# Four heads in four row groups of the array, with unused products over all rows in front of the row pairs

## The reference

```python
q = (x @ wq.T).reshape(B, S, 16, 8); k, v likewise       # 16 heads of 8
probs = softmax(einsum('bqhd,bkhd->bhqk', q, k) / sqrt(8))
out = einsum('bhqk,bkhd->bqhd', probs, v) @ wo.T
...
we = sum(where(sel == e, rw, 0))                          # top 2 of 8 experts
out += (silu(x @ w1[e].T) * (x @ w3[e].T)) @ w2[e].T * we
```

## Time and profile before

| | |
|---|---|
| median of 3 runs | 1235.07 us (1224.66 to 1239.53) |
| profiled execution | 1228.6 us, its span 1226.8 us |
| mean granted TensorE clock | 0.914 of full speed |
| busy: PE, DVE, ACT, POOL | 82%, 68%, 54%, 34% of the span |
| projection / attention / expert stage | 0 to 227, 227 to 985, 985 to 1227 us |

### The profile page before, as it was taken

One profiled execution on the slowest core, in us unless ns is written; L12 is line 12 of the kernel. 1 busy time (PEld: TensorE's weight loads), 2 busy tenths in 40 slices (PEclk: granted clock), 3 DMA queues, 4 the chain that ended last, 5 costly groups with the idle time before them and its releaser, 6 DMA issues. The chain is left out here.

```text
span 1226.8 us, 21943 instructions
## 1 busy us (share of the span) xinstructions
PE 1005.9 (82%) x5592; PEld 472.9 (39%) x5592; DVE 836.2 (68%) x1286; ACT 666.3 (54%) x1382; POOL 418.3 (34%) x767
## 2 busy tenths in 40 slices
PE   0156666999999999999999999999999968777850
PEld 0034442333333344344344344434443235554530
DVE  5667658789888778888888888888884013232552
ACT  1001111577777677777777777777776534333320
POOL 6103310010110143433433523524522434644576
PEclk9978776899999989999999999999998579988985
DMA  8954566010100110100101101101100012212342
GB/s 269 383 190 137 137 172 172 1 36 10 36 26 10 37 28 10 44 25 20 43 11 33 43 10 35 43 10 35 44 1 2 17 36 64 73 50 70 96 130 71
DMA packets 61944, 81.56 MB, mean 66 GB/s; under 512 B 8512, under 2 KB 39488, under 8 KB 61504
## 3 DMA queue, kind: packets, MB, share of 16 engines
q1 hardware_dynamic: 45808, 51.93, 14.8%
q10 hardware_dynamic: 11984, 20.59, 4.6%
q0 software_dynamic: 4096, 8.40, 2.3%
HBM read 32.12 MB, written 48.23 MB: 65 GB/s over the span
## 5 line engine op out<-in xcount | busy, mean ns | idle before, releaser
L1084 DVE TENSOR_REDUCE smax<-ps 128x2 f32<-128x1024 f32 x512 | 601.7, 1220 | 96.7 <-PE ps L1273 93.5
L853 ACT ACTIVATE prob<-ps 128x512 f32<-128x512 f32 x1024 | 528.8, 603 | 160.2 <-PE ps L1322 157.5
L1322 PE MATMUL ps<-qpack,kpack 34*128 34x512 f32 x1024 | 383.8, 458 | 23.6 <-ACT prob L853 11.7
L1273 PE MATMUL ps<-kpack,qpack 34*128 34x512 f32 x1024 | 314.2, 452 | 10.0 <-DVE smax L1084 9.3
L1322 PEld LDWEIGHTS ps<-qpack,kpack 34*128 34x128 f32 x1024 | 172.9, 189 | 297.2 <-ACT prob L853 250.2
L1332 PE MATMUL ps<-prob,vpad 128*32 128x512 f32 x2048 | 284.7, 629 | 0.0
L1273 PEld LDWEIGHTS ps<-kpack,qpack 34*128 34x128 f32 x1024 | 138.3, 189 | 41.3 <-DVE smax L1084 28.5
L450 POOL MEMSET qpack<- 2x2048 f32 x32 | 57.6, 1799 | 207.9 <-PE ps L1322 205.2
L1190 DVE TENSOR_TENSOR prob<-ps,prob 128x256 f32<-128x256 f32 x80 | 33.9, 424 | 104.9 <-ACT prob L906 104.0
L1498 PE MATMUL ps<-w,ws 128*128 x160 | 89.1, 642 | 15.3 <-ACT ws L899 14.5
L906 ACT ACTIVATE prob<-ps 128x256 f32<-128x256 f32 x80 | 30.8, 385 | 86.3 <-PE ps L1498 86.3
(11 more groups left out here) (211 smaller groups left out, 881.4 us busy)
## 6 DMA issues: line engine op xcount, KB each, us to landing
by_expert_rows<-prob ACTq DMA_DIRECT2D x4, 4864.0 KB, 30.9
q_parts<-qk SPq DMA_DIRECT2D x32, 256.0 KB, 3.8
k_parts<-qk SPq DMA_DIRECT2D x32, 256.0 KB, 4.0
kpack<-k_parts SPq DMA_DIRECT2D x32, 256.0 KB, 3.9
qpack<-q_parts SPq DMA_DIRECT2D x64, 128.0 KB, 3.3
vall<-by_expert_rows SPq DMA_DIRECT2D x80, 64.0 KB, 1.8
by_expert_rows<-vall SPq DMA_DIRECT2D x80, 64.0 KB
w<-w_t SPq DMA_DIRECT2D x3, 1024.0 KB, 10.1
```

The costliest lines, as they stand in the source:

```text
L853: act.activation(prob[:, v % RING, :], bank(col_bank(pos, kind)), ACT.Exp).then_inc(col_free, 1)
L1084: dve.tensor_reduce(smax[:, half, :, pair, qt, kh], ps[:, first:first + 2, :], AX_X, ALU.max).then_inc(row_free, 1)
L1273: ins = pe.matmul(bank(first + par), qpack[r:r + ROWS, slot, half, pair, qt * P:(qt + 1) * P], kpack[r:r + ROWS, slot, pair, kh * HALF:(kh ...
L1322: pe.matmul(bank(col_bank(pos, kind)), kpack[r:r + ROWS, slot, head // 2, kt * P:(kt + 1) * P], qpack[r:r + ROWS, slot, half, head // 2, : ...
```

## The change

CROSS becomes 24: three products of parts for four (low with low is left out), still with two rows for the maxima. Each head has its own 32-partition row group. Row pairs run over the 24 rows alone, so the clears go. In front of each row pair outside the opening, `keep_busy` issues one or two bfloat16 products over all 128 rows whose result the row pair overwrites. The last column product of a group moves, with the extra items, to the start of the next group, behind W. W's four increments become one. The seed on DVE and one of three Newton rounds go, for a power step on POOL. `save_x` runs one tile earlier.

```diff
-PARTS = 2
-CROSS = PARTS * PARTS * HD
+TERMS = 3
+CROSS = TERMS * HD
-ODD = 64
+LANE = 32
-PACK = 16 * 6
+PACK = 16 * 3 * HQ
...
 def save_parts(b):
+  if part == 0:   # both places of the high part in one DMA
+      both = (0, 2, 1) if w == 0 else (0, 3, 2)
...
+  else:
+      o = 2 if w == 0 else 1
+      sp.dma_start(rows[o * LANE:o * LANE + LANE, :], whole).then_inc(parts_out, 16)
 def load_k(n, slot):
-    for par in range(2):
+    for h in range(HQ):
+        sp.dma_start(kpack[LANE * h:LANE * h + CROSS, slot, :].bitcast(F32),
+                     of_head(k_parts, n, h)).then_inc(pack_in[slot], 16)
...
 def place_maxima(slot, half):
+    for part in range(PARTS):
+        sp.dma_start(qpack[CROSS + part:P:LANE, slot, half, :].bitcast(F32),
+                     mtr[16 * part:16 * part + 16, :]).then_inc(m_placed, 16)
...
-            def clear_maxima(slot):
...
+            gp.memset(kpack[:, :, :].bitcast(F32), 1.0).then_inc(pads, 1)
...
 def refill(i, slot, base, kind):
-    gp.wait_ge(col_full, base + (col_pos(UNITS - 1, kind) + 1))
-    gp.wait_ge(vpad_in, 2 * i + (2 + slot))
+    gp.wait_ge(pv_done, i * (2 * UNITS) + ((slot + 1) * UNITS + RING))
     gp.sem_inc(passed, 1)
-    clear_maxima(slot)
...
+                step(gp.tensor_tensor(rstd, var, power[:, :], ALU.pow))
...
-                gp.wait_ge(f_seed, t + 1)
-                for _ in range(3):
+                for _ in range(2):
...
-                if j % 4 == 3 and j + 1 < TILES_T:
+                if j % 4 == 2 and j + 2 < TILES_T:
                     save_x(j // 4 + 1)
...
+            def keep_busy(n, b):
+                for _ in range(n):
+                    pe.matmul(bank(b), busy[:, 0:P], busy[:, :], start=True, stop=True)
 def score_rows(p, slot, base, opening=False):
-    half, pair, qt, kh = p // 16, p % 16 // 8, p % 8 // 2, p % 2
+    half, pair, qt, kh = p // 16, 1 - p % 2, p % 16 // 4, p % 4 // 2
...
+    if not opening:
+        keep_busy(1 + p % 2, first)
+    for n in range(2):
+        r = (2 * pair + n) * LANE
+        ins = pe.matmul(bank(first + n), qpack[r:r + CROSS, slot, half, qt * P:(qt + 1) * P],
+                        kpack[r:r + CROSS, slot, kh * HALF:(kh + 1) * HALF], start=True, stop=True)
...
 def weigh_values(g, slot, base, kind):
-    ... .then_inc(pv_done, 1)
+    ins.then_inc(pv_done, HQ)
...
+            def last_of(g, job, slot, base, kind, t=None):
+                score_cols(4 * g + 3, 4 * g + 4, slot, base, kind)
+                for name in EXTRA[kind].get(g, ()):
...
 def group(g, i, slot, base, kind, before=None, t=None, opening=False):
+    if g > 0:
+        last_of(g - 1, job, slot, base, kind, t)
+    elif not opening:
+        last_of(15, job - 2, 1 - slot, *before)
...
     def rows(k):
...
+        else:
+            if g == 4 and k == 0:
+                pe.wait_ge(row_free, O_LAST)
+            keep_busy(1 + k, 2 - row_banks(O_LAST))
-    score_cols(4 * g, 4 * g + 1, slot, base, kind)
     rows(0)
-    score_cols(4 * g + 1, 4 * g + 3, slot, base, kind)
+    score_cols(4 * g, 4 * g + 2, slot, base, kind)
     rows(1)
-    score_cols(4 * g + 3, 4 * g + 4, slot, base, kind)
+    score_cols(4 * g + 2, 4 * g + 3, slot, base, kind)
     ...   # W of the group before, as it was
```

More of the change, by code:

```diff
@@ L344, in place_maxima @@
-            def place_maxima(slot, half):
[L346 to L350, removed]
+                            rows = dram[bass.ds(b * (NQ * TERMS * LANE) + j * (TERMS * LANE), TERMS * LANE), :]
+                            whole = qk2[LANE * j:LANE * j + LANE, w, part, :].bitcast(F32)
@@ L430, in _ @@
             gp.memset(ones[:, :], 1.0).then_inc(consts, 1)
+            gp.memset(power[:, :], -0.5).then_inc(consts, 1)
+            gp.memset(busy[:, :], 1.0).then_inc(consts, 1)
             gp.iota(iota_t[:, :], pattern=[[1, TILES_A]], base=0, channel_multiplier=0,
@@ L445, in _ @@
             gp.tensor_copy(run[:, 4, :], ebase[:, 0, :]).then_inc(consts, 1)
[L447 to L457 removed]
+            gp.memset(kpack[:, :, :].bitcast(F32), 1.0).then_inc(pads, 1)
+            gp.memset(vpad[:, :, :, :, :], 0.0).then_inc(pads, 1)
             gp.wait_ge(pads, 2)
[L459 to L461 removed]
             gp.memset(vpad[:, :, :, :, HD:HD + 1], 1.0).then_inc(pads, 1)
@@ L1143, in _, with dve_quad @@
             start += 2
-            def dve_quad(i, slot, own, last=False, t=None):
+            def dve_quad(i, slot, own, last=False):
                 base = i * (2 * ROW_ITEMS) + slot * ROW_ITEMS
@@ L1156, in dve_quad @@
                     split_maxima(0, following + (pair_pos(15) + 1), own + 3)
-                    maxima(16, 20, following)
-                    if t is not None:
-                        seed(t, own + 5)
-                    maxima(20, PAIRS - 2, following)
-                    finish_o(quad, 1, following + (O_LATE + 1), row_banks(O_LATE), own + (5 + extra))
+                    maxima(16, PAIRS - 2, following)
+                    finish_o(quad, 1, following + (O_LATE + 1), row_banks(O_LATE), own + 5)
                 else:
@@ L1165, in dve_quad @@
                     finish_o(quad, 1, O_LAST + 2, FINAL_BANK, own + 3)
-            with loop(dve, 0, 2) as i:
+            with loop(dve, 0, QUADS // 2 - 1) as i:
                 own = i * (2 * PER_QUAD) + start
@@ L1270, in score_rows @@
                     pe.wait_ge(row_free, base + (pos - 1))
-                for par in range(2):
-                    r = par * ODD
-                    ins = pe.matmul(bank(first + par), qpack[r:r + ROWS, slot, half, pair, qt * P:(qt + 1) * P],
-                                    kpack[r:r + ROWS, slot, pair, kh * HALF:(kh + 1) * HALF], start=True, stop=True)
+                if not opening:
[4 more added lines that the diff above has]
+                                    kpack[r:r + CROSS, slot, kh * HALF:(kh + 1) * HALF], start=True, stop=True)
                 ins.then_inc(row_full, 1)
```

126 lines of the change are left out of this document (46 added, 80 removed).

## The result

The changed kernel takes 1348.83 us (median of 4 runs, 1345.99 to 1351.42) where the kernel before, on the same chip, takes 1230.79 us (1224.66 to 1239.53): a ratio of 1.0953, with a 95% interval from 1.0871 to 1.1034. The profiled execution took 1351.42 us, its span is 1349.6 us, its mean clock 0.908. Against the profiled execution of before that is +122.8 us, where the forecast was +112.

What follows compares the result with a forecast made beforehand. The prediction took a loop through TensorE and ACT, 2.71 us per group, to bound the kernel. It summed 1228.6 + 134 - 14 - 8 = 1341 us, with an 8-in-10 range from 1205 to 1372.

Steps and rivals of the forecast that it cites:

- The mechanism: Attention groups: changes of array shape around the unused products make TensorE the bound, 3.23 us per group instead of 2.70.
- Rival 1: Between a group's moved last column and its third column: switches around unused products are free, 0 per group, 1207 us; chance 0.22.
- The passes: Attention groups outside the opening: shape changes and unused products add 0.53 us in each of 253 groups, +134 us.
- D: Block of one unused product, behind the moved last column: weight load, stream and drain take 0.36 us.
- DD: Block of two unused products, ahead of a group's second row pair: takes 0.58 us.
- the extra items add what they added: 0: Maxima, projection and logits, now between the moved last column and the first unused product: no additional cost, 0.
- The clock: Last quad: unused products keep the higher clock level, -14 us; the other hole gives 0, or -5 if it goes.
- The term of the last quad: Last quad, without row pairs: unused products keep the higher level, a group taking 2.70 us instead of 4.06, -14 us.
- The opening has no dummies: Opening of attention: it gets no unused products; no cost was put on it.
- the hole in quad 4: Lower clock after a stall ending at 422.20 us, which the change leaves: 0, or -5 if it goes.
- rival 3: Attention: the clock falls despite unused products, as 24-row products fill less; 5.75 us per group, +126 more, 1467 us; chance 0.06.
- The expert stage: Behind attention: earlier save_x, no DVE seed, fewer saved copies and Newton steps give about -8 us, bounds -13 and +1.

Runs made afterwards that it cites:

- the last one: Kernel before plus the expert edits and a block of two unused products in the last quad alone; 1310.89 us against 1337.99, ratio 0.9818.

## Why the prediction was right, and by how much its terms were off

**The mechanism** is the one forecast: TensorE became the bound through its changes of shape, and the marks named for it are there. Period 3.15 (forecast 3.23), 0.42 after c3' (0.43), idle time of DVE per maximum 233.5 / 512 = 0.46 us (0.4), no wait of TensorE for ACT before c2. The kernel without the blocks (2.69) and the one with blocks of the pair's shape (2.69) show that neither the layout nor the number of products is the cause. Rival 1 (free switches) is refuted by the rows above: a block costs its streams and some 0.10 us, where rival 1 needed switches under 0.02 us each.

**The passes, +134 forecast, about +120 measured.** The thirteen quads at full clock cost 7.5 us each where 16 x 0.53 is 8.5; sixteen of them would be 120. Two errors of size hide in that. D takes 0.32 and DD 0.53, not 0.36 and 0.58: entry and exit of a block are 0.32 - 0.215 = 0.105 us together, not the 0.15 that I read off float32 transposes. The plain period rose by 0.455 instead of 0.53 (115 us over 253 groups), and groups whose passes had slack before rose by only 0.3 to 0.4 (2.78 to 3.16 where one quad follows another). Against that stands the step "the extra items add what they added: 0". It was wrong: the groups with a turn rose from 2.91 to 3.66, 0.29 more than the others, which comes to about 5 us in the thirteen quads at full clock, since a turn beside other items cost less. I had followed the semaphores and TensorE's order, and not counted the ring's banks: an item that takes one between c3' and c0 makes c1 wait for the first exponential in place of c2. The experiment with the items first gives the 0.29 back (3.37), and those thirteen quads as a whole 4.3 us.

**The clock, -14 forecast, about +15 measured.** The term of the last quad was right: 49.2 us at 1.00; 15 won. Two steps failed. "The opening has no dummies" was read as no cost. In quad 0 the clock fell at 224 and came back at 275: eight groups of 5.55 us or more and a ninth of 4.38, instead of 3.15, +21. And for the hole in quad 4 I had written 0 or -5; it cost 9 more: it began with a shorter stall (1.12 us at 474.55, where before had 2.40) and lasted from 476.5 to 510.7, with groups of 5.55 to 7.44. This is rival 3's fall of the clock in two places; that it comes from the fewer rows isn't shown. Its period at the lower level was given as 5.75 and is 5.55, and I counted on full-array products to shut it out everywhere, though in the opening there are none. Nor do they bring the clock back soon once it is lost: in quad 0 they run from 231.7 on, and it stayed at 0.50 for 43 us more, TensorE busy for 97% of the window:

```profile
229.10:275.20 46.10, 44.80 (x159) 10.67 (x161) 21.60 (x21) 19.61 (x36) 0.00 (x0) 0.50 0.02 5
```

The kernel without unused products shows how close it was: without them the fall is the rule. The Trainium skill, "TensorE: Matmul & The Clock Gate" (Part 1), has the throttled state as the default that activity releases. The trace agrees in its direction; that an engine busy 94% of the time stays in it (the kernel without unused products) is this case's finding. What sets off the fall in the opening stays open.

**The expert stage, -8 forecast, -9.9 measured.** TensorE's waits for ACT before L1498 of before (14.5 us, 18 times) are one of 0.9 us at L1477 now, and POOL's 64 loads stay as long a queue (60.6 us busy and 32.8 idle; the earlier trace rows have 60.8 and 35.7). The power step takes 1.05 us, between the 0.20 and the 2 assumed. On one chip the stage took 247.3 us in the kernel before with unused products, and 232.6 and 233.5 in the two kernels with the expert edits (clock 0.83, 0.82 and 0.83). That speaks for the edits and against a mere shift of the rows' arrival, though the first of the three is from the traced execution of 1547.73 us; the one run with the edits alone was clouded by its chip, and which of them brings the gain wasn't tried apart. The stage also depends on the quad in front of it. The last quad and the stage of the kernel with the items first and products of the pair's shape:

```profile
956.30:1013.10 56.80, 56.00 (x298) 18.00 (x300) 7.89 (x13) 32.91 (x67) 24.38 (x59) 0.64 0.03 11
1013.10:1241.20 228.10, 153.50 (x788) 99.44 (x788) 82.95 (x226) 73.12 (x194) 130.51 (x240) 0.82 0.28 79
```

With the same edits and no long stalls the stage takes 235.6 us behind a last quad of 43.3, 231.8 behind 49.2, 228.1 behind 56.8 and 221.3 behind 72.9: a shorter last quad gives about half of its gain back. Behind a last quad as long as before's 56.6 the edits are thus worth 13 to 14 us (241.7 to 228.1), at the lower bound of -13, and since the last quad is 7.4 us shorter than before's, some 4 us are lost again here. Which work carries over isn't shown. **The projection stage**, 0 with bounds of -3 and +4, gave -2.3.

**The sum.** 134 - 14 - 8 = +112 against +122.8: passes -14, clock +29, expert stage -2, projection -2. The total lies near by luck, in part: two errors of opposite sign stood against each other; the clock's was the larger. Had the clock done as I wrote, the kernel would have taken some 1320 us.

## What to carry to other kernels

An unused product of another shape has three prices: its stream (0.215 us here), the entry into and exit from its block (0.10 us), and the work beside it that it cuts apart (two passes where one stood); give it a place with slack, in one block and not in two, and count which bank of a ring each moved item takes. A change of layout like this one can cost the clock, and a busy share of 94% gave no warning of it: look at the granted clock by window, in the openings and tails above all, where the filling work is missing. Before crediting a remedy such as this, cost the part of the kernel that it doesn't reach.

## What the runs showed of the hardware

**Rows and the clock.** In all ten traces of kernels with the 24- and 26-row products (nine kernels) attention began at the lower level (first period 4.06, clock 0.50 from between 224.0 and 227.4 on). The four with 34-row products (before, with unused products, with the expert edits, and the last one) began it at 1.00 (first period 2.60 or 2.61). The opening (the row pairs ahead of quad 0 and the first group) has no unused products in any of them. How long the lower level lasted differed: to 238 or 239 with one block of two, to 242 with one product in front of every row pair, to 251 and 275 with the same three products, to 256 and 306 with the 24-row ones, to 270 with one product in every second place, to 408 with none. Nor is it sure at the end: the last quad was at 1.00 in the changed kernel and fell (period 5.53) in the one with the items first, which has the same unused products. The two groups of kernels differ in more than the rows (row groups, order, clears), and no run tried the rows alone. Why, and what in the products the clock answers to, isn't settled.

**Chips.** The kernel before took 1235 and 1238 us on two of the four chips of the experiments, and 1356 and 1338 on the two others. On these two, the five kernels traced all had long stalls at the turn of the loop over quads, most of them in every second quad. ACT and TensorE in the last experiment's kernel, in one of them:

```profile
725.73 0.27 ACT L827 ACTIVATE mtr<-ps 32x128 f32<-32x128 f32 x1 [3.60 <-remote]
...
726.05 0.79 PE L1325 MATMUL ps<-qpack,kpack 34*128 34x512 f32 x1 [3.38 <-ACT mtr L827]
```

TensorE waits for ACT, and ACT for something that the profile can't name ("remote"). DVE stands too, and the column product behind it lasts 0.79: the clock fell. Groups of 4.15 us follow. That quad took 56.4 us, where its like before take 47.0 (835.1 to 882.1). What ACT waits for there stays open.
